# Expert sums in another PSUM bank, additions and expert rows of a fused Trainium2 kernel placed at other units

## The reference

```python
z = layernorm(x)                                   # 1024 rows of 256
scores = sigmoid(z @ gate.T)                       # 8 experts
sel = top_2(scores + expert_bias)
out = (silu(z @ shared_w1.T) * (z @ shared_w3.T)) @ shared_w2.T
for e in range(8):                                 # for the rows that chose e
    r = bfloat16(z * score_e)
    out += (silu(r @ w1[e].T) * (r @ w3[e].T)) @ w2[e].T
x = x + tanh(g_ffn[1]) * out
```

## Time and profile before

| what | value |
|---|---|
| median of 3 runs | 190.18 us (189.53 to 190.3) |
| the profiled execution | 190.67 us |
| its span, first to last instruction | 188.8 us |
| PE busy | 170.0 us, 90% of the span, 1204 products |
| DVE busy | 153.0 us, 81% |
| ACT busy | 113.6 us, 60% |
| POOL busy | 94.6 us, 50% |
| chain that ended last | PE 61%, ACT 16%, DMA 7%, DVE 7% |
| TensorE clock granted | full until the last slice of 40, where 0.8 |

### The profile page before, as it was taken

One profiled execution on the slowest core, in us unless ns is written; L12 is line 12 of the kernel. 1 busy time (PEld: TensorE's weight loads), 2 busy tenths in 40 slices (PEclk: granted clock), 3 DMA queues, 4 the chain that ended last, 5 costly groups with the idle time before them and its releaser, 6 DMA issues.

```text
span 188.8 us, 3740 instructions
## 1 busy us (share of the span) xinstructions
PE 170.0 (90%) x1204; PEld 115.2 (61%) x1204; DVE 153.0 (81%) x463; ACT 113.6 (60%) x293; POOL 94.6 (50%) x157
## 2 busy tenths in 40 slices
PE   7989999998999999989579879978989899999981
PEld 7957666667665555556356656655658557655640
DVE  0789989984599989989999999979874997748644
ACT  2465034833342446753699899998799796652630
POOL 1079999994999331510643306333304569294000
PEclk9999999999999999999999999999999999999998
DMA  5979976100000000000000000000000097875953
GB/s 162 330 213 354 382 316 239 68 0 3 0 2 0 0 2 0 3 0 0 0 3 2 0 3 2 3 0 3 0 0 3 17 177 90 166 131 106 174 149 111
DMA packets 22770, 15.18 MB, mean 80 GB/s; under 512 B 17664, under 2 KB 21344, under 8 KB 22368
## 3 DMA queue, kind: packets, MB, share of 16 engines
q1 hardware_dynamic: 22112, 13.94, 27.9%
q10 hardware_dynamic: 640, 1.02, 1.6%
HBM read 9.68 MB, written 1.07 MB: 57 GB/s over the span
## 4 chain that ended last, share of the span: by engine, by line
PE 61%; ACT 16%; DMA 7%; DVE 7%; issue 4%; SPq 2%; DVEq 0%
PE PS L1801 9%; ACT R L745 6%; PE PS L1434 5%; DMA CT<-ctxr 5%; PE PS L1431 5%; PE PS L1430 5%; PE PS L1535 4%; ACT R L740 4%; PE PS L1819 4%; PE PS L1648 4%; PE PS L1505 4%; PE PS L1469 3%; PE PS L1632 3%; PE PS L1457 3%; DMA R<-R 3%
## 5 line engine op out<-in xcount | busy, mean ns | idle before, releaser
L1116 DVE TENSOR_REDUCE SM<-PS 128x8 f32<-128x1024 f32 x16 | 18.9, 1216 | 2.0 <-PE PS L1618 1.8
L1632 PE MATMUL PS<-CON,R 128*128 128x128 f32 x128 | 18.4, 276 | 1.4 <-ACT R L745 1.3
L354 POOL TENSOR_TENSOR R<-CT 128x512 f32<-128x512 f32 (+1 forms) x16 | 16.0, 1001 | 6.4 <-DMA CT<-ctxr 6.4
L541 POOL TENSOR_SCALAR R<-QT,SM 128x256 bf16<-128x256 f32 x32 | 16.0, 517 | 5.9 <-DVE SM L1195 5.6
L745 ACT ACTIVATE R<-PS 128x512 f32<-128x512 f32 x32 | 18.4, 606 | 0.2 <-PE PS L1632 0.2
L1317 DVE TENSOR_TENSOR R<-R,PS 128x512 bf16<-128x512 f32 (+1 forms) x17 | 11.7, 686 | 7.6 <-PE PS L1801 5.6
L1801 PE MATMUL PS<-R 128*128 128x512 bf16 x64 | 16.4, 379 | 0.8 <-DMA R<-R 0.8
L496 POOL TENSOR_TENSOR R<-R,ROW 128x256 f32<-128x256 f32 x8 | 5.8, 737 | 21.6 <-ACT R L682 10.9
L550 POOL TENSOR_TENSOR R<-R 128x640 f32<-128x640 f32 (+1 forms) x12 | 15.0, 1284 | 2.8 <-DVE T_R L1045 2.8
L1632 PEld LDWEIGHTS PS<-CON,R 128*128 128x128 f32 x128 | 14.3, 140 | 3.1 <-issue 2.7
L883 ACT ACTIVATE R<-PS 128x512 f32<-128x512 f32 x17 | 10.1, 595 | 9.7 <-PE PS L1801 9.5
(11 more groups left out here) (168 smaller groups left out, 447.0 us busy)
## 6 DMA issues: line engine op xcount, KB each, us to landing
WST<-w SPq DMA_DIRECT2D x3, 1024.0 KB, 12.7
T_R<-lagged SPq DMA_DIRECT2D x2, 768.0 KB, 7.7
X<-x SPq DMA_DIRECT2D x2, 512.0 KB, 4.9
CT<-ctxr SPq DMA_DIRECT2D x2, 512.0 KB, 8.3
y<-X SPq DMA_DIRECT2D x8, 128.0 KB, 2.0
WQP<-wqp ACTq DMA_DIRECT2D x1, 512.0 KB, 7.1
WKV<-wkv SPq DMA_DIRECT2D x1, 512.0 KB, 10.0
R<-sw SPq DMA_DIRECT2D x3, 128.0 KB, 4.3
```

The costliest lines, as they stand in the source:

```text
L354: return eng.tensor_tensor(KV[:, h % RING, lo:hi, 0:32].rearrange("p c (i j) -> p c i j", i=4), k[:, :, 0:4].unsqueeze(3).to_broadcast([P, ...
L541: nc.gpsimd.tensor_scalar(XB[:, u % XS, j, :], MX[:, b, :], GG[:, b, e:e + 1], 1.0, ALU.mult, ALU.mult).then_inc(e_xb, 1)
L1116: V_.tensor_reduce(MX1[:, b % 2, 8 * c:8 * c + 8], S4[:, 8 * c:8 * c + 8, :], AX.X, ALU.max, negate=True).then_inc(a_mx, 1)
L1632: ins = TR(PS[:, 4 + k % 2, P * h:P * h + P], SS[:, b % 2, 4 * k + h, :], I)
```

## The change

It has three parts. The sums of group 1 lie in the banks 7 and 6 instead of 6 and 0; PE's wait on x4 before the third block of unit 9 is gone, and a wait on o_n for 37 (the second mark of the last block) stands before its first. The four additions of group 0 no longer stand together after product 9 and its rows, but one each after the products 10, 11, 12 and 13 (behind the rows of the same place). The rows of DVE and ACT of the runs 10 to 13 stand together after unit 8, those of 14 after unit 9 and those of 15 after unit 10.

```diff
-ROWS_AT = {1: (4, 5), 2: (6,), 3: (7,), 6: (8,), 7: (9,), 8: (10,), 9: (11, 12), 10: (13,), 11: (14,), 12: (15,)}
+ROWS_AT = {1: (4, 5), 2: (6,), 3: (7,), 6: (8,), 7: (9,), 8: (10, 11, 12, 13), 9: (14,), 10: (15,)}
...
-            return PS[:, ((0, 1), (6, 0))[g][j // 2], DM * (j % 2):DM * (j % 2) + DM]
+            return PS[:, ((0, 1), (7, 6))[g][j // 2], DM * (j % 2):DM * (j % 2) + DM]
...
                 for u in ROWS_AT.get(v, ()):
                     if u not in BOTH:
                         third_rows(u)
-                if v == NE + 1:
-                    g = 0
+                if 0 <= v - NE - 2 < GT:
+                    b = v - NE - 2
                     dve.wait_ge(e_acc, NE + 1)
-                    for j in range(GT):
-                        b = GT * g + j
-                        V_.scalar_tensor_tensor(X[:, b, :], acc(g, j),
-                                                TG[:, 3:4], X[:, b, :], ALU.mult, ALU.add).then_inc(x4, 1)
+                    V_.scalar_tensor_tensor(X[:, b, :], acc(0, b), TG[:, 3:4], X[:, b, :], ALU.mult, ALU.add
+                                            ).then_inc(x4, 1)
...
                 if v == 0:
                     pe.wait_ge(y_d, LATE)
                 elif e == 0:
+                    pe.wait_ge(o_n, ONT * (NB - 1) + 2)
                     pe.wait_ge(m_ge, NG)
                 for j in range(GT):
-                    if e == 0 and g == 1 and j == 2:
-                        pe.wait_ge(x4, 2)
                     if v == UNITS - 1 and j % 2 == 0:
                         pe.wait_ge(last_ht, j // 2 + 1)
```

## The result

| | before | after |
|---|---|---|
| median of 4 runs each | 190.24 us (189.53, 190.18, 190.3, 190.46) | 188.8 us (188.7 to 188.85) |
| ratio | | 0.993, 95% interval 0.9903 to 0.9956 |
| the profiled execution | 190.67 us, span 188.8 | 188.83 us, span 186.9 |

Predicted were 188.6 us and a range of 188.0 to 189.5.

The account below looks back on a forecast made before the run. TensorE (PE), busy 90% of the span, was taken as the bound, with two stalls in the expert part. 0.62 + 0.99 = 1.61 us off the median of 190.18 gave 188.57 us; range 188.0 to 189.5.

Parts of the forecast that it names:

- First stall: In unit 9's output products PE waits for two DVE additions before reusing a bank; moving the banks gains 0.62 us.
- part (c) alone would leave the bank's wait: Moving only the rows was said to leave PE's wait for the bank in unit 9 standing.
- Second stall: Before unit 17's hidden products PE waits for the last DMA transpose to land; issuing it earlier gains 0.99 us.
- gave it 0.09: Rival, chance 0.09: the stall before unit 17 is smaller without the profiler; gain 1.12 us, time 189.06.
- They crowded the last transpose before: The stores queued behind the last transpose were said to make it land in 4.94 us, where the median is 3.3.
- Part (a) alone would gain nearly nothing: Moving only the banks would gain nearly nothing, since the chain before unit 17 starts from DVE's rows, not PE.
- Part (b), nothing: On DVE, additions one per unit after products 10 to 13 were said to cost nothing.
- spare of 0.22 us: At products 11 to 13, DVE's product and addition take 1.08 us of the 1.30 us beat, 0.22 to spare.
- The burst of four rows: DVE's rows of runs 10 to 13 fill its idle before product 9, taking 2.2 us, ending near 169.6.
- The rival by the lock of the shared port: DVE's four rows each wait out a POOL row, taking 3.3 us; within the DVE-bound rival, chance 0.09, 189.2 us.
- the backlog of eight transposes: Rivals on the DMA queue: mild at 1.67 us a transpose, 189.5 us, chance 0.09; heavy, 191.2 us, chance 0.03.
- The sum: Both stalls' gains added, 0.62 + 0.99 = 1.61 us, giving 188.57 us against the median of 190.18.

Follow-up runs that it names:

- (c) alone: Kernel before with only the DVE and ACT rows of runs 10 to 15 moved to their new places; median 188.82 us, ratio 0.9946.
- (a) with (c): Kernel before with the new banks and wait and the moved rows, the four additions still together; median 188.72 us, ratio 0.9936.
- (a) alone: Kernel before with only group 1's sums in banks 7 and 6 and the wait on x4 replaced by one on o_n; median 189.11 us, ratio 0.9972.
- before held: Kernel before with one line more: the first store waits until the last transpose has landed; median 189.92 us, ratio 1.0011.
- e12_wide_warm: Kernel before with 13 matmuls of ones of 256 columns at PE's start instead of 26 of 128; 190.7 us, ratio 1.0043.
- (a) with (b): Changed kernel with the old row places put back, leaving the new banks and the spread additions; median 188.76 us, ratio 0.9954 to before.

## Why the prediction was right, and where it was not

- **First stall, 0.62 us, part (a).** Right in size: with the wait gone the eight records are in one piece. The lower cluster of before lies 0.62 above (c) alone and 0.72 above (a) with (c), and no kernel with the new rows has the stall. But "part (c) alone would leave the bank's wait" was wrong. It stood there without a sum: (c) leaves one row instead of two ahead of the additions, and with a row of 0.35 us two of them fitted ahead of PE's need. The change has two cures for one stall.
- **Second stall, 0.99 us, part (c).** This is the term that was mis-sized. It is right for the execution that was profiled, which is one of the upper cluster (190.67), but I charged it to every execution. In four sets of runs of the kernel before 29 of 95 are in the upper cluster. In the others, as far as the profiled executions of (a) alone and of before held tell (3.2 and 3.0 us), it lands at about 180.9, ahead of its due time of 181.69, and there is nothing to gain. I had a hint and gave it 0.09: the profiled execution was 0.49 above the median.
- **Its cause.** "They crowded the last transpose before", of the stores, was wrong: held back, they changed nothing. A fetch of PE's instructions is shown to lengthen transposes, and where it was moved the stall moved with it. What makes the fetch come at another time in each execution stays open.
- **"Part (a) alone would gain nearly nothing"**: wrong. It gains 0.4 in the two runs of three without the second stall, and 0.5 between the upper clusters.
- **Part (b), nothing**: right beside (c), and its spare of 0.22 us is in the trace to the digit. That it gives 0.36 beside the old rows, by taking the additions out of product 10's way, the prediction did not ask.
- **The burst of four rows and the rest of (c)**: right. 1.99 us for 2.2, a pitch of 1.41 for 1.40, last issue 175.13 for 175.3. The rival by the lock of the shared port (3.3 us) didn't happen; the backlog of eight transposes neither, all eight landed in 3.3 to 3.4. What spoke for the backlog, 1.67 us for each of the first four, held the fetch at 155.31 and the two transposes that it lengthened; in `e12_wide_warm`, without it, the first four are charged 0.75 x 7.59 / 4 = 1.42 us, like the later ones. (Its landing is 177.2 + 4.94 = 182.1 and not 182.0, which changes nothing.)
- **The sum.** 1.61 against a measured 1.44 of the medians, and so near by luck: three of the four runs of before in that comparison were of the upper cluster. Against the 25 runs of before the change is worth 0.6 to 0.7 us in the lower cluster, some two executions of three, and 1.5 to 1.6 in the upper; (a) with (c), equal to it in time, measured 0.83 us, 0.64%, on the medians. So the range and "faster" held, and the likeliest size was too large for a typical run. What the change really gives is as much steadiness as speed: in no trace with the new rows has a long landing reached PE, since the last transpose is issued 2.3 us earlier. In the trace of (a) with (c) one did strike the runs 14 and 15 (4.9 and 4.4), and PE never waited.

## What to carry to other kernels

Where a stall is a DMA's landing that is far above that DMA's median, ask first whether it is there in every execution: list the single times before and after, and look for clusters, since one profile shows one of them. The stall that came and went was cured here by issuing the transfer earlier than its worst landing, which was cheaper than to find what strikes it. Put the span beside each time as well: what a time has more outside its span is no stall of the program's. And try the parts of a change alone: of three edits here one alone did nearly all, and the other two together did as much in two executions of three, by another way.

## What the hardware showed that was not expected

- PE's instructions come in by DMA, 16 KB at a time, and one packet of 0.9 to 1.5 us makes a DMA transpose in flight 0.6 to 1.8 us longer (3.9 to 5.0 in all instead of 3.0 to 3.5); in the trace of before by a single late one of its sixteen landings, in others by all. Only a fetch that began 0.6 us before the landing, in the trace of the changed kernel, did nothing. Taking 13 matmuls away at PE's start moved the last two fetches 6 us and more, and a stall of 1 us with them.
- An issue on SP's queue was drawn out as well, where a fetch had lengthened the transposes ahead of it: 1.86 and 2.23 us for a transpose instead of 1.25.
- DVE's and POOL's rows side by side cost DVE 0.50 us a row in the burst of four (1.99 / 4) instead of 0.35, and POOL's sixteen took 7.56 instead of 7.51 us: neither waits out the other's whole instruction here. A single row beside POOL's took 0.35 us in the traces of (c) and of (a) with (c), and 0.67 in that of the changed kernel, in the same place.
